# One state tile for two heads, 64-row products, and an inverse of eight units at a time in an attention and expert kernel

## What is computed

```python
q, k, v = silu(conv(x @ w_q)), silu(conv(x @ w_k)), silu(conv(x @ w_v))      # 16 heads, DK = 64, DV = 128
q, k = l2norm(q), l2norm(k)
def step(S, inp):                       # once per token, 512 tokens per sequence, 16 sequences
    S = S * exp(g_t)
    mem = einsum('bhk,bhkv->bhv', k_t, S)
    delta = (v_t - mem) * b_t
    S = S + einsum('bhk,bhv->bhkv', k_t, delta)
    o_t = einsum('bhk,bhkv->bhv', q_t * scale, S)
y = rms_norm(o) * norm_w * silu(x @ w_g)
return y @ w_out
```

## Time and profile before

| | us |
|---|---|
| median of 3 runs | 4765.86 |
| lowest, highest | 4765.37, 4773.78 |
| span of the profiled execution | 4761.7 |
| what lies around the span (median less span) | about 4.2 |
| PE busy, share of the span | 98% |
| DVE, ACT, POOL busy | 87%, 71%, 66% |

### The profile page before, as it was taken

The page is one execution under the profiler, slowest core; times in us unless marked ns, Lnnn a source line. Parts: engine busy times, 40 slices in busy tenths (PEclk is TensorE's granted clock), DMA queues, the critical chain, the costliest instruction groups (busy, mean ns, idle before and its releaser), DMA issues. The chain is left out here.

```text
span 4761.7 us, 140986 instructions
## 1 busy us (share of the span) xinstructions
PE 4665.0 (98%) x44336; PEld 3733.8 (78%) x44336; DVE 4138.2 (87%) x9914; ACT 3397.1 (71%) x10287; POOL 3152.1 (66%) x4511
## 2 busy tenths in 40 slices
...
PEclk9999999999999999999999999999999999999899
...
DMA packets 206732, 212.94 MB, mean 45 GB/s; under 512 B 17218, under 2 KB 180180, under 8 KB 206036
## 3 DMA queue, kind: packets, MB, share of 16 engines
...
## 5 line engine op out<-in xcount | busy, mean ns | idle before, releaser
L1074 DVE SCALAR_TENSOR_TENSOR cv<-ps_a,wqkv,cv 128x511 f32<-128x511 f32 (+2 forms) x1536 | 1145.8, 746 | 181.6 <-ACT cv L1067 161.0
L1279 POOL TENSOR_TENSOR bm<-bat,mask 128x256 f16<-128x256 f32 x1536 | 1029.5, 691 | 0.6
L1059 PE MATMUL ps_a<-xin,wqkv 128*128 128x512 f32 x2048 | 1002.8, 612 | 3.0 <-DVE bat L1256 1.5
L1329 ACT ACTIVATE m<-b 128x256 f16<-128x256 f32 x1536 | 597.2, 389 | 376.2 <-PE b L1324 376.2
L1067 ACT ACTIVATE cv<-ps_a,wqkv 128x512 f32<-128x512 f32 x512 | 352.0, 688 | 554.3 <-PE ps_a L1059 554.1
L1340 DVE TENSOR_TENSOR tt<-tt,b 128x256 f16<-128x256 f16 x1536 | 635.4, 414 | 115.4 <-PE b L1335 114.8
L1382 ACT CAST tt<-bu 128x256 f16<-128x256 f32 x1536 | 578.2, 376 | 1.2 <-PE bu L1377 0.5
L1514 PE MATMUL ps_a<-wout,yT 128*128 128x256 f32 x2048 | 548.3, 390 | 0.5 <-ACT yT L1508 0.5
L1059 PEld LDWEIGHTS ps_a<-xin,wqkv 128*128 128x128 f32 x2048 | 349.6, 191 | 250.6 <-issue 250.6
L1207 PE MATMUL ps_b<-wgate,xin 128*128 128x256 f32 x2048 | 494.9, 384 | 0.2 <-DVE vtok L1230 0.2
L1256 DVE SCALAR_TENSOR_TENSOR bat<-ps_a,w,dec 128x256 f32<-128x256 f32 x1024 | 435.4, 477 | 40.5 <-DVE w L1126 22.4
...
## 6 DMA issues: line engine op xcount, KB each, us to landing
xin<-xT_scratch SPq DMA_DIRECT2D x128, 512.0 KB, 4.0
grow<-g_scratch SPq DMA_DIRECT2D x256, 256.0 KB, 4.6
gam<-g_scratch SPq DMA_DIRECT2D x256, 96.0 KB, 2.8
...
```

The source lines that it names most:

```text
L1059: ins = pe.matmul(ps[:], wqkv[:, k, j * P:(j + 1) * P], xin[p][:, k, :], start=k == 0, stop=k == KT - 1)
L1074: s.done(dve.scalar_tensor_tensor(y[:, r:], ps[:, 0:T - r], tap[:, j, TAPS - 1 - r:TAPS - r], y[:, r:], ALU.mult, ALU.add), f"a_tap{j}{r}")
L1279: s.done(pool.tensor_tensor(half_of(bm[:, l, units(g), :], l, 1), half_of(bt[:, units(g), :], l, 1), half_of(c["mask"][:, l, :].unsqueeze( ...
L1329: s.done(act.mul(half_of(m1[:, l, units(g), :], l, 0), half_bank(bank, l), -1.0), f"b_Me{l}{g}")
```

## The change

- The state becomes one tile [128, 128], head 0 in rows 0 to 63 and head 1 in rows 64 to 127. `c_KS` is now four products, eight fp32 instructions: for each head 64 rows of keys times the head's 64 rows of state (128 columns), then the same with queries. The two heads write into two banks, the halves of the new tile `cc` (banks of `cs` and `co`). The queries' part is taken out of `c_O`.
- `c_SU` is merged into `c_O`: the growths of both heads are accumulated into one 128x128 area, then the attention products follow.
- `c_S` handles 128 columns in place of 256.
- The inverse handles all eight units per step, 512 columns per evacuation in place of two times 256: `b0` (`inverse`) holds transposes, M, V and the correction of half 0; `bu` holds U and the correction of half 1. `b1` (`side`) becomes the bank of `c_Z`, the state's growth and the turned output.
- `c_y` is split: `c_t` on DVE multiplies the output by the gate (one instruction of 128x256), and `c_y` on POOL multiplies by the root-mean-square factor (two of 128x128). `yy` becomes two tiles. The squares `c_sq` come before `c_t`, and the `cc` banks are held from `c_KS` to `c_t`.
- The order of the slot is new. `b_qT`, `b_sq1`, `b_n1`, `b_eps`, `b_kqs`, `b_sg1` and `b_vT1`, among others, move to the next lag; the number of slots stays.

```diff
 SLOT_ORDER = """
...
+    b_bm20.2 y_bn0 y_bn1 x_mv.5 x_ve.5 b_bm41.2 c_m1.3 b_Me2.2 a_silu1.1 x_rs.5 b_V2.2 b_kT.1 b_E0.1 b_sg1.2 b_bm51.2
+    c_R2.3 b_sq0.1 c_Z2.3 d_ln.1 y_mv k_out.1 y_ve b_Ve2.2 c_u2.3 b_U2.2 b_M3.2 c_acc0.3 b_n0.1 c_p1.3 b_bm30.2
+    b_Ue2.2 b_kk0.1 b_ss.1 b_bm40.2 b_Me3.2 b_rc.1 k_mix.1 c_O2.3 y_rs b_V3.2 x_sh.5 c_y1.3 b_w1.1 b_ev00.1 a_proj2.1
+    c_sq2.3 x_y0.5 x_y1.5 b_E1.1 a_cv2.1 c_yT1.3 c_S2.3 d_add.1 b_ev01.1 b_Ve3.2 y_sh b_U3.2 c_yTe1.3 b_bm50.2
+    d_turn.1 c_t2.3 b_Ue3.2 d_spt.1 d_beta.1 b_kw.1 c_m2.3 b_M4.2 c_KS3.3 b_ktok.1 a_tap21.1 d_cum.1 c_R3.3 d_rmm.1
+    c_out1.3 c_p2.3 y_xT.1 b_Me4.2 y_xf0 b_root.1 c_Z3.3 c_acc1.3 a_tap22.1 b_hi1.2 b_V4.2 a_tap23.1 b_Ve4.2 c_y2.3
+    c_u3.3 b_vT1.2 a_tanh2.1 a_proj3.1 c_O3.3 a_cv3.1 d_cums.1 b_vtok1.2 c_sq3.3 a_silu2.1 a_tap31.1 c_t3.3 b_kqs.2
+    b_U4.2 k_end.1 b_lo1.2 b_M5.2 x_bn0.4 a_tap32.1 d_rows.1 c_yT2.3 c_m3.3 b_Me5.2 b_Ue4.2 c_p3.3 b_g0.1 b_V5.2
+    a_tap33.1 c_yTe2.3 c_y3.3 b_U5.2 c_yT3.3 b_Ve5.2 x_x0.5 a_tanh3.1 x_x1.5 b_Ue5.2 b_diag0.1 c_yTe3.3 c_out2.3 y_xf1
+    b_gam.1 b_t20.1 a_silu3.1 c_acc2.3 b_tg0.1 x_y2.5 b_diag1.1 x_y3.5 b_P0.2 b_P1.2 b_R0.2 b_R1.2 b_kk1.1 b_sg0.1
+    x_bn1.4 b_F0.2 b_F1.2 b_qT.2 x_x2.5 b_ev11.1 c_Z0.2 b_T0.2 b_ev10.1 c_out3.3 c_acc3.3 b_hi0.1 c_u0.2 b_sq1.2
+    c_sq0.2 b_T1.2 c_O0.2 a_proj1 d_abs a_cv1 d_max b_Tq.1 d_exp b_n1.2 d_th a_proj0 b_Tf.1 c_S0.2 b_eps.2 c_KS1.2
+    c_t0.2 a_cv0 b_t21.1 b_M0.1 a_tap11 b_sel a_tap12 b_vT0.1 b_Me0.1 a_tap13 b_bm00.1 b_bm01.1 c_R1.2 x_bn2.4 c_Z1.2
+    a_tap01 b_V0.1 x_bn3.4 b_bm10.1 c_m0.2 b_vtok0.1 k_turn c_u1.2 b_Ve0.1 a_tanh1 b_U0.1 b_bm11.1 x_x3.5 b_Ue0.1
+    c_O1.2 k_cp a_tap02 k_prod c_ws.2 b_M1.1 b_gend.1 c_S1.2 b_g1.1 c_sq1.2 a_tap03 c_p0.2 b_Me1.1 c_t1.2 y_turn
+    b_bm21.1 a_tanh0 c_y0.2 b_V1.1 a_silu0 c_yT0.2 c_yTe0.2 b_U1.1 b_bm31.1 b_tg1.1 c_KS2.2 b_Ue1.1 b_Ve1.1 b_M2.1
+    c_out0.2 b_lo0.1
...
-        state = sb("state", [P, 2, DV])
+        state = sb("state", [P, DV])
...
+        of_heads = cc[:].rearrange("p (h e) -> p h e", h=2)
+        chain, out = of_heads[:, :, 0:DV], of_heads[:, :, DV:2 * DV]
+        inverse, side = halves
+        zz, grown_state = side[:, 0:2 * DV].rearrange("p (h e) -> p h e", h=2), side[:, 2 * DV:3 * DV]
...
+            [("b_Tq", "b_T0")], [(f"b_U{l}", f"b_Ue{l}") for l in range(NLEV)] + [("b_P1", "b_T1")],
+            [(f"c_yT{m}", f"c_yTe{m}") for m in range(CH)] + [(f"c_Z{m}", f"c_S{m}") for m in range(CH - 1)]
+            + [(f"c_Z{CH - 1}", f"c_u{CH - 1}")],
+            [("c_O0", "c_t0")] + [(f"c_KS{m}", f"c_t{m}") for m in range(1, CH)],
...
+                    if (yield f"b_M{l}"):
+                        s.need(pe, i, f"b_bm{l}0", f"b_bm{l}1", f"b_Ve{l - 1}" if l else "b_Tf")
+                        for u in range(NU):
+                            ins = pe.matmul(half_bank(inverse, l)[:, u], bm[:, l, u, :], even[:, u], start=True, stop=True)
+                        s.done(ins, f"b_M{l}")
...
-                            ins = pe.matmul(cs[:, 0:2 * DV], kqs[p][:, k_in, m - 1, :],
-                                            state[:].rearrange("p h e -> p (h e)"), start=True, stop=True)
+                            for h in range(2):
+                                rows = slice(h * DK, (h + 1) * DK)
+                                pe.matmul(chain[:, h, :], kqs[p][rows, k_in, m - 1, :], state[rows, :], start=True, stop=True)
+                            for h in range(2):
+                                rows = slice(h * DK, (h + 1) * DK)
+                                ins = pe.matmul(out[:, h, :], kqs[p][rows, q_in, m - 1, :], state[rows, :],
+                                                start=True, stop=False)
                             s.done(ins, f"c_KS{m}")
...
+                        if m < CH - 1:
                             for h in range(2):
-                                ins = pe.matmul(cs[:, h * DV:(h + 1) * DV],
-                                                ktok[p][:, m, 2 * h:2 * h + 2, :].rearrange("p b e -> p (b e)"), uu[:, h, :],
-                                                start=True, stop=True)
-                            s.done(ins, f"c_SU{m}")
+                                pe.matmul(grown_state, ktok[p][:, m, 2 * h:2 * h + 2, :].rearrange("p b e -> p (b e)"),
+                                          uu[:, h, :], start=h == 0, stop=h == 1)
                         for h in range(2):
-                            e = slice(h * DV, (h + 1) * DV)
-                            if m:
-                                pe.matmul(co[:, e], kqs[p][:, q_in, m - 1, :], state[:, h, :], start=True, stop=False)
-                            ins = pe.matmul(co[:, e], at[:, 2 * m + h, :], uu[:, h, :], start=m == 0, stop=True)
+                            ins = pe.matmul(out[:, h, :], at[:, 2 * m + h, :], uu[:, h, :], start=m == 0, stop=True)
...
+                if (yield f"c_t{m}"):
+                    s.need(dve, i, f"c_sq{m}", f"b_sg{m // 2}")
...
+                    s.done(dve.tensor_tensor(yy[m % 2][:], out, sg[p][:, m, :].rearrange("p (h e) -> p h e", h=2), ALU.mult),
+                           f"c_t{m}")
...
                     for h in range(2):
-                        e = slice(h * DV, (h + 1) * DV)
-                        ins = dve.scalar_tensor_tensor(yy[:, h, :], out[:, e], col(rms, h), sg[p][:, m, e], ALU.mult,
-                                                       ALU.mult)
+                        ins = pool.tensor_scalar(yy[m % 2][:, h, :], yy[m % 2][:, h, :], col(rms, h), None, ALU.mult)
```

178 lines of the change are left out of this document (80 added, 98 removed).

## The result

The kernel with the change takes 4946.71 us (4942.95 to 4948.66, four runs) against 4766.38 us (4765.37 to 4773.78, four runs) on the same chip: the ratio is 1.0377, 95% interval 1.0363 to 1.0392. The forecast was 4708 with 4672 to 4800, so the change is slower by 180 us where I expected 58 less.

The account below looks back on a forecast made before the run. PE's instruction stream was taken to set the 33.67 us item; -0.62 of stream plus 0.17 of waits gave 33.22, -0.45 per item, x 128 = -58 us, so 4708 us from 4765.9, range 4672 to 4800.

Parts of the forecast that it names:

- PE's stream, -0.62 to 33.05: PE's work per item: state products -0.39, 64-row groups before fp32 +0.17, fewer fp16-to-fp32 changes -0.40; 33.05 us.
- The state products, -0.39: Per item on PE: old `c_KS` (1.29) and `c_O` queries' part (1.32) out, three 64-row groups (2.22) in.
- The pair step at 128 columns: Two heads' 64-row products on PE run at once, 0.11 us per pair, between bounds 0.11 and 0.22.
- the 0.30 of switching: Each group of 64-row products on PE costs 0.30 us beyond its paired stream, for filling and leaving.
- Rival 3: 64-row pairs on PE do not overlap at 128 columns: +0.87 us per item, 4877 us; chance 0.04.
- Waits of 0.17: PE's waits at narrow places of the new order, taken as 0.17 us per item in all.
- this place, with 0.13: At `c_O1` behind `c_Z1`, `b_V0`, `b_U0`: PE has 0.48 us of work against a chain of 0.61, short by 0.13.
- The seam (`c_out0`, `b_V2`): Where two slots meet on PE: ACT in time by 0.07 us if its instructions overlap, otherwise 0.2 late.
- I cost it at nothing: POOL's new `c_y` multiplications, 2.4 us per item at 0.3 each, fit its 11.4 of idle time; cost zero.
- `load_gam` now waits for the later `b_kqs` [...] nothing: The DMA load of `gam` waits longer, with half a slot left until `b_gam`; cost zero.
- filling and draining slots [...] are unchanged: Slots' filling and draining and the expert phase keep their time; all 128 items change by -0.45 us each.
- Rival 1: ACT's longer evacuations are late for PE: +0.48 us per item, +61 in all, 4827 us; chance 0.16.

Follow-up runs that it names:

- this base: The changed kernel with the gate's weights loaded ahead of `load_gam` and `c_y` as one POOL instruction for both heads: 4798.5 us, ratio 1.0067.

## Why the prediction was wrong, point by point

- **PE's stream, -0.62 to 33.05: its largest term held.** The state products, -0.39, were measured at -0.42 (undoing them lengthens the steady item by that; the first weight loads of neighbouring groups are in it). The pair step at 128 columns (taken at 0.11 between 0.11 and 0.22) and the 0.30 of switching held: 0.74 per group against 0.75. Rival 3 is out. The whole stream without waits was not measured.
- **Waits of 0.17: mis-sized by 0.40 an item, about 50 us.** The steady item with one POOL instruction is 33.62, which is 0.57 above the sum's 33.05. The timeline of PE in that kernel shows where most of it lies:

```profile
2419.98 0.71 PE L1422 MATMUL b<-rr,tinv 128*128 128x128 f32 x4
2420.53 0.40 PE L1331 MATMUL b<-m,tt 128*128 128x64 f16 x8
2420.77 0.40 PE L1345 MATMUL bu<-tt,m 128*128 128x64 f16 x8
2421.16 0.71 PE L1439 MATMUL b<-uu,ktok 128*128 128x128 f32 x4
...
2430.62 0.40 PE L1331 MATMUL b<-m,tt 128*128 128x64 f16 x8
2431.00 1.96 PE L1061 MATMUL ps_a<-xin,wqkv 128*128 128x512 f32 x4
...
2433.89 0.39 PE L1407 MATMUL cc<-state,kqs 64*128 64x128 f32 x4
2434.21 1.13 PE L1506 MATMUL ps_a<-wout,yT 128*128 128x256 f32 x4
2435.18 0.61 PE L1422 MATMUL b<-rr,tinv 128*128 128x128 f32 x4
```

  The growth and `c_O1` start 0.39 behind a group of 0.23, so 0.15 is lost; I had named this place, with 0.13. `a_proj2` behind `b_ev00` (a bank that both use) loses about 0.15 in the same way, and `c_Z1` takes 0.55 where it takes 0.45 elsewhere; these two I had not found. `c_out1` behind the tiled products takes 0.97 against 0.87, but of this 0.10 the sum had 0.08. The remaining 0.15 is in pieces of 0.05 or less that I haven't traced. The seam (`c_out0`, `b_V2`) was not late. So PE loses what the shorter stream gives, and the item is as long as before (33.67 in the earlier trace rows). This is where the expected 58 us went. Of the moves that I tried, none that took one of these waits away made the steady item of this base shorter.
- **"I cost it at nothing": the first failed step, 92 to 97 us.** I took 0.3 for a multiplication on POOL between 0.17 and 0.70; the nearest row was a whole instruction of four times the size with 0.696, and the measured 0.61 for a quarter of the size lies next to it. What mattered more: I compared with POOL's idle time (11.4 per item) and looked at the distance of `c_y` to `c_yT` for m = 0 and 1 only. For m = 3 the order has `b_U5` alone between them, and the chain O, squares, `c_m`, `c_p`, `c_y` is serial: idle time of an engine says nothing on a chain. The total of `c_y`'s time, 1.2 per chunk, was a cost for one chunk of four.
- **"`load_gam` now waits for the later `b_kqs` [...] nothing": the second failed step, about 50 us.** I looked at who needs `gam`, and not at what is queued behind that wait on SP: x and the weights of the gate. Seven times PE waited about 5 us for them.
- **The same item 128 times, "filling and draining slots [...] are unchanged": the third, about 30 us.** The last eleven items run the residual's steps beside them, and I gave them the -0.45 of a steady item too. In the kernel after they are 2.7 us longer than its steady items, in the base with both causes mended 2.3, and there they add 24.1 us over the kernel before (394.7 against 370.6); with the forecast's 5 us less that makes 29. In the kernel after, DVE's results ended 19.0 of PE's 26.0 us of waits in ten of these items. Moving the residual's steps behind what PE waits for gives back 0.96 per item. What of the remaining 1.3 is order and what is work of DVE (from 28.9 to 31.0 us per item) wasn't tried. The beginning, the drain and the expert phase of the kernel after add another 9.4 us.
- **Rival 1** had the right sign and the wrong reason: the large waits of PE are those for POOL, for a DMA behind SP's queue and, in the last items, for DVE. ACT's evacuations can be 0.2 longer each for 12 us.
- **The shares,** by the ratios 1.0377, 1.026 and 1.0067: 56 (weights) + 92 (POOL) + 32 (what is left) = 180. By the medians the first two are 52 and 97. Against the forecast of -58 the 32 is 90 more: about 50 are the waits, 29 the last eleven items, and the rest lies at the beginning and the end.
